# A recurrence on one core: the first half of the features released early, the leak's product in halves, loop bodies moved to the end

## What is computed

```python
def _L1_cond_ref(x, h0, Wx, Wh, b):
    xw = jnp.einsum('ntd,dh->nth', x, Wx) + b
    def step(prev_h, xw_t):
        next_h = jnp.tanh(xw_t + prev_h @ Wh)
        return (next_h, next_h)
...
def _L3_cond_ref(h_t, z, W, b, alpha):
    Wh = W[:, :D]
    Wz = W[:, D:]
    leak = 1.0 - alpha
    def step(h, z_t):
        gate = jax.nn.sigmoid(h @ Wh.T + z_t @ Wz.T + b)
        h_new = jnp.tanh(h * leak + gate * z_t)
        return (h_new, h_new)
    _, hs = jax.lax.scan(step, h_t, jnp.swapaxes(z, 0, 1))
...
x = x + _L0_cond_ref(x, cond_1024, L0_cond_W1, L0_cond_b1, L0_cond_W2, L0_cond_b2)
x = x + _L1_cond_ref(x, cond_1024, L1_cond_Wx, L1_cond_Wh, L1_cond_b)
...
x = x + _L3_cond_ref(cond_1024, x, L3_cond_W, L3_cond_b, L3_cond_alpha)
```

## Time and profile before

| | us |
|---|---|
| median of 3 runs | 1987.21 |
| lowest, highest | 1985.87, 1987.57 |
| the profiled execution | 1989.81 |
| its span in the profile | 1988.0 |
| its mean granted TensorE clock | 0.994 |
| TensorE busy | 1950.2 (98%) |
| VectorE busy | 1110.3 (56%) |
| ScalarE busy | 813.3 (41%) |
| GpSimd busy | 140.3 (7%) |

### The profile page before, as it was taken

One profiled execution on the slowest core, in us unless ns is written; L12 is line 12 of the kernel. 1 busy time (PEld: TensorE's weight loads), 2 busy tenths in 40 slices (PEclk: granted clock), 3 DMA queues, 4 the chain that ended last, 5 costly groups with the idle time before them and its releaser, 6 DMA issues. The chain is left out here.

```text
span 1988.0 us, 45588 instructions
## 1 busy us (share of the span) xinstructions
PE 1950.2 (98%) x18112; PEld 1149.9 (58%) x18112; DVE 1110.3 (56%) x2361; ACT 813.3 (41%) x1701; POOL 140.3 (7%) x144
## 2 busy tenths in 40 slices
PE   8999989999999999999999999999999999999997
PEld 6999954444444444444444444444455555888886
DVE  5666656644896645111111147555655664788887
ACT  4444444422121434343333345322333332566665
POOL 0000000000000000121111012111111110000000
PEclk8999999999999999999999999999999999999999
DMA  7033337765342533999988855433322353101111
GB/s 299 14 127 137 128 139 202 214 175 141 108 180 94 172 104 103 236 217 218 219 203 204 180 201 167 157 90 90 96 86 86 101 123 128 45 3 44 42 42 45
DMA packets 281902, 266.36 MB, mean 134 GB/s; under 512 B 225991, under 2 KB 233293, under 8 KB 275086
## 3 DMA queue, kind: packets, MB, share of 16 engines
q1 hardware_dynamic: 270942, 228.73, 39.9%
q0 software_dynamic: 10800, 35.40, 6.5%
HBM read 153.70 MB, written 56.36 MB: 106 GB/s over the span
## 5 line engine op out<-in xcount | busy, mean ns | idle before, releaser
L1080 PE MATMUL sh_p<-xh,arena 128*128 128x512 f16 x2048 | 609.5, 379 | 1.6 <-PEq L1767 1.5
L1080 PE MATMUL sh_p<-xl,arena 128*128 128x512 f16 x1024 | 388.3, 379 | 0.0
L1080 PEld LDWEIGHTS sh_p<-xh,arena 128*128 128x128 f16 x2048 | 200.3, 98 | 243.9 <-issue 2.6
L1095 PE MATMUL p<-sh_h_hi,arena 128*128 128x512 f16 x1024 | 304.5, 379 | 0.0
L1878 DVE SCALAR_TENSOR_TENSOR ro_hs<-ro_h,fac,ro_hs 128x512 f16<-128x512 f32 x71 | 53.3, 751 | 302.1 <-ACT ro_hs L1864 266.7
L1255 ACT CAST sh_h_hi<-sh_half_h 128x512 f16<-128x512 f32 x128 | 79.0, 618 | 347.0 <-DVE sh_half_h L1630 347.0
L1821 PE MATMUL ro_py<-arena,ro_ht 128*128 x852 | 197.0, 381 | 3.1 <-DMA ro_ht<-ro_hs 3.1
L1249 ACT ACTIVATE sh_sig<-sh_p,fac 128x512 f32<-128x512 f32 x128 | 87.6, 685 | 263.7 <-PE sh_p L1080 263.7
L1095 PE MATMUL p<-sh_h_lo,arena 128*128 128x512 f16 x512 | 194.0, 379 | 0.0
L1080 PEld LDWEIGHTS sh_p<-xl,arena 128*128 128x128 f16 x1024 | 100.3, 98 | 120.9 <-issue 0.3
L1627 DVE SCALAR_TENSOR_TENSOR sh_half_h<-sh_sig,sh_p 128x512 f32<-128x512 f32 x128 | 87.5, 684 | 145.9 <-ACT sh_sig L1249 145.8
(11 more groups left out here) (287 smaller groups left out, 3125.2 us busy)
## 6 DMA issues: line engine op xcount, KB each, us to landing
stage<-in_shared_w SPq DMA_DIRECT2D x29, 768.0 KB, 5.2
routed_rows<-xres SPq DMA_DIRECT2D x71, 256.0 KB
stage<-in_norms_r SPq DMA_DIRECT2D x16, 1024.0 KB, 5.1
stage<-in_routed_w SPq DMA_DIRECT2D x16, 1024.0 KB, 4.8
stage<-in_norms SPq DMA_DIRECT2D x14, 1024.0 KB, 4.9
arena<-x SPq DMA_DIRECT2D x12, 1024.0 KB, 5.9
rnn_xs<-in_x SPq DMA_DIRECT2D x8, 1024.0 KB, 19.1
x<-xres SPq DMA_DIRECT2D x16, 512.0 KB, 2.6
```

Source lines behind the costliest of these rows:

```text
L1080: mm = nc.tensor.matmul(p1[u % P1][:], arena[:, w:w + P], x[slot(gl)][:, :, k, :], start=(j == 0), stop=(j == 3 * KD - 1))
L1095: mm = nc.tensor.matmul(p2[m][:], arena[:, w:w + P], h[n % 2][:], start=(i == 0 and j == 0), stop=(i == HID - 1 and j == 2))
```

## The change

Five edits:
1. In `leaky` the state products stand in another order. First, as before, all outputs with the first half of `h_hi` (16 products). Then only the first half's outputs: with the second half of `h_hi` (8). Then all outputs with the first half of `h_lo` (8), the first half's outputs with the second half of `h_lo` (4), and the first release. The second half's outputs with the second halves of `h_hi` and `h_lo` (12) come last, and then the second release.
2. `hd` is computed in two halves, each right behind the `h_lo` of its half, and without its own wait on ScalarE; `arg` waits for its half.
3. The first recurrence's further rounds are put behind those of the second one, at the end of each engine's program. Its branch is now taken only if a further round is needed, and has no prefetch hint. The second recurrence's branch stays as it was.
4. A register of its own for the loop's flag in the further rounds.
5. Three of the blocks' kinds (recurrences, shared, routed) are opened with `no_gpsimd_drain=True`, which leaves out GpSimd's drain at the block's end.

```diff
+                def further_rounds():
+                    with nc.body(again, parent=checked, valid_engines=[eng.engine]):
+                        with eng.register(f"{name}_{eng.engine.name}_further") as more:
+                            eng.reg_load(more, running[0:1, 0:1])
+                            with eng.Fori(2, SEGS + 2) as r:
...
+                if gate:
+                    eng.br_ne(go, 0, on_true=again, on_false=over)
+                    further[eng.engine] = further_rounds
+                else:
+                    eng.br_eq(go, 0, on_true=over, on_false=again).branch_hint(settled)
+                    further_rounds()
+                    ready["further"][eng.engine]()
                 nc.switch_bb(over)
...
-        with nc.Block() as block:
+        with nc.Block(no_gpsimd_drain=True) as block:
...
-                sp.sem_inc(hd_ready, 1)
+                sp.sem_inc(hd_ready, parts)
...
+                        if leaky:
+                            a, b = own
+                            fine = (s - ROUGH * CHUNK_STEPS) * 2
+                            pe.wait_ge(hi_ready, s * 2 + 1)
+                            state(every, a, wr_hi, h_hi)
+                            state(every, a, wr_lo, h_hi)
+                            pe.wait_ge(hi_ready, s * 2 + 2)
+                            state(a, b, wr_hi, h_hi)
+                            state(a, b, wr_lo, h_hi)
+                            pe.wait_ge(lo_ready, fine + 1)
+                            state(every, a, wr_hi, h_lo)
+                            pe.wait_ge(lo_ready, fine + 2)
+                            state(a, b, wr_hi, h_lo, True).then_inc(pre_ready, 1)
+                            state(b, b, wr_hi, h_hi)
+                            state(b, b, wr_lo, h_hi)
+                            state(b, b, wr_hi, h_lo, True).then_inc(pre_ready, 1)
...
-                                dve.wait_ge(hd_ready, s + 1)
+                                dve.wait_ge(hd_ready, s * parts + h + 1)
...
+                                if leaky:
+                                    nc.vector.tensor_tensor(hd[:, part, BATCH:], hist[p][:, part, cols],
+                                                            decay[:, part].unsqueeze(2).broadcast_to([P, KD // parts, LANES]), ALU.mult).then_inc(hd_ready, 1)
...
-                        if leaky:
-                            dve.wait_ge(hi_ready, (s + 2) * parts)
-                            nc.vector.tensor_tensor(hd[:, :, BATCH:], h_hi[:, :, BATCH:] if rough else hist[p][:, :, cols],
-                                                    decay[:].unsqueeze(2).broadcast_to([P, KD, LANES]), ALU.mult).then_inc(hd_ready, 1)
```

30 lines of the change are left out of this document (15 added, 15 removed).

## The result

| | before | after |
|---|---|---|
| median of the runs, us | 1987.57 (5 runs) | 1975.01 (5 runs) |
| lowest, highest | 1985.87, 1991.25 | 1971.73, 1975.64 |
| the profiled execution | 1989.81 | 1971.73 |
| its span in the profile | 1988.0 | 1969.9 |

The ratio is 0.9919 with an interval of 0.9906 to 0.9932, that is 13.5 to 18.7 us less. The prediction was 1972.5 (1968.5 to 1978.8), from a sum of 14.7 us.

A forecast was written before the change was run, and what follows sets the result against it. TensorE was taken to bind the middle part, step-by-step waits the two recurrences. The second recurrence's 12.3 us plus 2.4 at the transition made 14.7 us less, giving 1972.5 us against the median, range 1968.5 to 1978.8.

The forecast's parts named there:

- TensorE's work: Second recurrence, constant code: TensorE's 48 state and 13 input products need 2.85 us and bind; 31 plain intervals give 4.0 us.
- the release: Second recurrence: TensorE's leg from first state product to first sigmoid falls from 1.57 to 1.37 us; constant ring 2.78.
- x_hi to xo: Second recurrence's register loop: x_lo waits for x_hi, then xo and gz follow; ring 2.97 us, 36 intervals give 4.3 us.
- plain interval: Second recurrence, sigmoid to sigmoid, not at a chunk's start: 4.0 us gained in constant code, 4.3 in the loop.
- chunk starts: Second recurrence: input products wait for the last x_lo; 0.18 us less each with constants, 0.13 in the loop, 1.6 each.
- the transition: End of the first recurrence: TensorE's 3.97 us branch shrinks, SyncE is last, next block starts 2.4 us earlier, 2.8 at most.

The follow-up runs named there:

- e4_light: The kernel before with only the light closings (no GpSimd drain at the end of three kinds of block); 1991.68 us median, ratio 1.0012.
- e5_same: The kernel before once more, without any edit; one execution, 1988.66 us.
- e6_xo_first: The changed kernel with xo ahead of x_lo in the second recurrence's full round, except at a chunk's last step; 1970.89 us median, ratio 0.9906.
- e12_both: The changed kernel with the loop's twelve chunks written out and xo ahead of x_lo within a chunk of the full round; 1968.04 us median, ratio 0.9896.
- e8: The changed kernel once more, without any edit; 1973.68 us median, ratio 0.9921.
- e7: The changed kernel with the twelve chunks of the second recurrence's register loop written out with constants; 1967.28 us median, ratio 0.9889.
- e9: The changed kernel with a spare copy of the leak's first half product on VectorE ahead of the second h_lo; 1976.75 us median, ratio 0.9936.
- e11: The changed kernel with ordinary closings (GpSimd's drain kept) in place of the light ones in three kinds of block; 1973.25 us median, ratio 0.9918.

## What to carry over

Follow a step round through each engine, write down each ring's length, and when the longest is cut, take the second longest as the new period; three rings (TensorE's work, the release, x_hi to xo) gave here the mean of each kind of plain interval to about 0.01 us; chunk starts were less sure. What stands ahead of a release should be only what the release needs, and an extra instruction on a neighbour is free exactly as long as that neighbour's idle time lasts. Where a step's wait value is formed in a register ahead of the critical instruction, writing the loop out can be worth a good part of what a reordering gives: here 5.7 us, beside 10.35 of the new order.

## What the runs showed of the hardware

**The granted clock goes with the scatter.** All fourteen profiles have the first recurrence at 223.72 us, and the second recurrence repeats to 0.1 us for the same program. What differs between executions is the stretch behind a start of work. Windows: stretch, busy times of PE, PEld, DVE, ACT, POOL, then the granted TensorE clock. First some 40 us behind the start of the routed part, in the kernels before, e4_light and after:

```profile
780.00:820.00 40.00, 36.32 (x161) 15.90 (x160) 11.09 (x14) 14.92 (x20) 8.54 (x10) 0.96 0.79 160
```
```profile
780.00:820.00 40.00, 34.66 (x148) 14.98 (x146) 9.71 (x12) 14.31 (x19) 9.26 (x10) 0.91 0.79 166
```
```profile
780.00:820.00 40.00, 36.95 (x172) 16.55 (x170) 10.47 (x13) 15.64 (x22) 10.85 (x11) 1.00 0.94 202
```

Over all fourteen: with 0.91 there (three profiles) the routed part takes 379.0 to 380.4 us, with 0.96 (three) 376.5 to 377.3, with 1.00 (eight) 374.4 to 375.7. Kernels with the old branch and with the new one are in each class, so no part of the gain is claimed from it. The size fits too: in 40 us a clock of 0.96 is 1.6 us of full clock less and 0.91 is 3.6, and the means of these two classes are 1.8 and 4.6 us above that of the class at 1.00. The totals go the same way: of 31 executions of the kernel before, those at a mean clock of 0.993 average 1996.2 us (two), at 0.995 1990.5 (twelve), at 0.996 1987.7 (fourteen). That the clock is the cause and not the effect of work that came late is not shown by this. The first 40 us of the program behave alike; kernel before, then its second execution (e5_same):

```profile
0.00:40.00 40.00, 33.63 (x282) 23.32 (x283) 20.58 (x50) 19.34 (x37) 0.78 (x6) 0.87 0.94 369
```
```profile
0.00:40.00 40.00, 34.20 (x335) 25.11 (x336) 22.27 (x54) 19.97 (x38) 0.78 (x6) 0.96 0.94 368
```

With 0.87 to 0.91 the first recurrence's first fp32 tanh is at 42.2 to 42.6 (four profiles), with 0.96 at 40.1 to 40.5 (the other ten). There the time does not follow the clock in its size: 0.87 is no later than 0.91. What decides which of them an execution gets stays open.

**The same clock takes back a part of a shorter pause.** Behind the transition TensorE works for some us at a granted clock of 0.50, which is 1.2 GHz. First the kernel before (e5_same), then after:

```profile
270.00:272.00 2.00, 0.30 (x4) 0.33 (x5) 0.00 (x0) 0.33 (x1) 0.00 (x0) 0.93 0.04 14
272.00:274.00 2.00, 2.00 (x20) 1.76 (x19) 1.57 (x3) 2.00 (x4) 0.20 (x1) 0.50 0.52 141
274.00:276.00 2.00, 2.00 (x7) 0.79 (x8) 2.00 (x4) 2.00 (x5) 0.00 (x0) 0.72 1.03 416
```
```profile
268.00:270.00 2.00, 1.28 (x20) 1.13 (x20) 0.97 (x2) 1.72 (x3) 0.20 (x1) 1.00 0.81 211
270.00:272.00 2.00, 1.41 (x4) 0.59 (x5) 2.00 (x4) 2.00 (x5) 0.00 (x0) 0.64 0.92 350
272.00:274.00 2.00, 2.00 (x7) 0.65 (x5) 1.76 (x3) 2.00 (x4) 0.00 (x0) 0.51 0.95 374
```

Before, the half clock begins right behind the barrier and falls for its first part on twenty small 128x128 products, where TensorE would soon wait for its inputs anyway. After, these twenty run at full clock, TensorE waits 1.02 us for VectorE, and the half clock falls on the products of 128x512, which count:

```profile
270.59 1.01 PE L1111 MATMUL sh_p<-xh,arena 128*128 128x512 f16 x2 [1.02 <-DVE xl L1374]
...
274.18 0.59 PE L1111 MATMUL sh_p<-xh,arena 128*128 128x512 f16 x2
```

Measured from the last fp32 tanh, the first of these products comes 3.2 us earlier than in e5_same (270.59 - 263.93 against 273.99 - 264.15), and the fourth pair 2.1 us (274.18 against 276.48). In this pair the difference thus shrinks from 3.2 to 2.1. On the means it shrinks from 2.8 to 2.4, since the old kernels, too, have a part of the half clock on these products.

That the clock takes it is borne out by two more runs. In e6_xo_first and e12_both, whose code is that of the changed kernel up to the second recurrence, the clock does not fall behind the transition:

```profile
272.00:274.00 2.00, 2.00 (x11) 0.82 (x10) 1.94 (x3) 2.00 (x4) 0.00 (x0) 1.00 0.97 392
```

Their first of these products starts 6.66 us behind the last fp32 tanh as in the changed kernel, the fourth pair already at 8.60 and not at 10.25. From the last fp32 tanh to the end of the first shared part they take 513.4 us, for 514.5 in the four profiles of the same code with the whole half-clock stretch on these products (after, e8, e7, e9): 1.1 us is what it costs there.

**One step of the changed kernel stands out.** In both of its executions the second interval of the loop's second chunk is 3.23 and not 2.96; with e6's edit, without the loop and with the ordinary closings (e11) it is gone. VectorE stands idle there ahead of x_lo, and the profile names nothing that it waits for:

```profile
1800.03 0.48 DVE L516 SCALAR_TENSOR_TENSOR leaky_x_lo<-leaky_xs,lk_px,leaky_x_hi 128x256 f16<-128x256 f16 x1 [0.38 <-issue]
```

It is worth 0.3 us, and its cause stays open.
